# Every fourth block of one-hot columns made on ScalarE in two passes

## The chip, the cores and the metric

One NeuronCore of a Trainium2 chip. The metric is the time in microseconds that the device takes for one execution of the program. Before the change the median of three runs is 751.01 us (750.84 to 751.55).

## The reference

2048 samples, each with 40 categorical fields and 16 dense features. Every field has a table of embeddings of 32 numbers; 7 tables have 1000 rows, 10 have 1250, the others 12500 or 125000. All pairs of fields interact through a 32x32 matrix of their own, and three dense layers follow:

```python
e = jnp.stack([tbl_f[ids[:, f]] for f in range(40)], axis=1)
vi, vj = e[:, I, :], e[:, J, :]                  # 780 pairs i < j
z = jnp.einsum('bke,kef,bkf->bk', vi, W, vj)
h = jnp.concatenate([z, dense_ctx], axis=1)
h = jnp.maximum(h @ W_top1 + b_top1, 0.0)        # 796 -> 512
h = jnp.maximum(h @ W_top2 + b_top2, 0.0)        # 512 -> 256
y = h @ W_top3
```

## The kernel before

The batch is cut into four chunks of 512 samples, and the 40 fields into ten groups of four, so that a group of transposed embeddings, `e_t`, is one tile of 128 partitions by 512 samples. Seven groups are fetched by indirect DMAs that GpSimd issues (L331), are turned on TensorE (L481) and copied out of PSUM by ScalarE (L368).

The other three groups, h = 0, 1, 2, are the twelve smallest tables. They aren't fetched but looked up with matrix products. The ids of a chunk lie in `hot_sb`, the same on every partition, as fp16. For block n of 128 table rows, VectorE compares these ids with the row number of each partition and writes 1 or 0 into a tile `one_hot` (128 partitions, 4 fields, 512 samples, bf16; L425). TensorE multiplies it with the block of the table, which is kept as three bf16 parts: 12 matmuls for a block with four fields (L465), all of a group summed in the one PSUM bank `x_ps`. The groups have 8, 10 and 10 blocks, so there are 28 blocks for each chunk and 112 in all. Blocks 8 and 9 of group 1 hold one field only.

`one_hot` has three slots (HOT_SLOTS, L29). The tile of block number m goes into slot m % 3, so its maker waits until TensorE is through with block m - 3. `steps_of` (L122) writes one list of steps by hand, and every engine walks that list and does its own part in this order. In it each one-hot tile stands right behind the look-up of the block two before its own (L143 to L153). The steps of the pair products (`gen`, L484, with VectorE's multiplication at L438, and `red`, L514, which sums the products into the bank `z_ps`) fill the rest. VectorE's part of a burst of `gen` is one or two multiplications of 128x1024; TensorE and VectorE are coupled by three slots of `t_ps` and six of `prod`.

Where the look-ups stand: all 28 blocks of chunk 0 come first, one behind another, with nothing between them but ScalarE's copies of the three finished groups. The look-ups of chunk k + 1 stand between the bursts of chunk k, one or two to a burst, by the tables in `between` (L89 to L116). In chunk 0 they are spread over bursts 20 to 42, in chunks 1 and 2 they stand at bursts 25 to 29, 36 to 42 and 45 to 52. Chunk 3 has none.

When the last one-hot tile of a chunk is made, SP loads the ids of the next chunk over `hot_sb` (L305 to L309), and VectorE waits for them at the first tile of the next chunk (L415, L416).

ScalarE does the copies out of PSUM, in the order of the list: `e_t` (L368), the two hidden layers (L373, L377), and, after every eighth `red`, the full bank `z_ps` (L393). TensorE's next `red` into that bank waits for it:

```python
if s == 0 and n > 0:
    pe.wait_ge(z_read, chunk * Z_BANKS + r // Z_SLOTS)
```

Of the kernel before, what the change touches and what calls it, by code (L numbers as in the profile page):

```python
# [26 lines left out]
EARLY_TURNS = list(range(HOT_GROUPS, PER))  # L27
TABLE_PARTS = 3
HOT_SLOTS = 3  # L29

# [39 lines left out]

def hot_pieces(k, h, blocks):
    return [("hot", k, h, n) for n in range(blocks[h])]


def layer1_pieces(k, m):
# [94 lines left out]
def tower_kernel(nc, idx_lay, tables, w_lay, w1_lay, b1, w2, b2, w3, dense_t, ident_in, select_in, hot_ids,  # L172
# [18 lines left out]
    one_hots = [step[1:] for step in steps if step[0] == "one_hot"]  # L191
    one_hot_no = {s: n for n, s in enumerate(one_hots)}

    looked_up_to = {s: sum(o[2] < blocks[o[1]] - 1 for o in one_hots[:n + 1]) for n, s in enumerate(one_hots)}
    in_tail = {("h1", chunks - 1, m): m for m in range(M1)} | {("h2", chunks - 1, m): M1 + m for m in range(M2)}
    items = [(k, c) for k in range(chunks) for c in GATHERED]
# [7 lines left out]
    with ExitStack() as ctx:  # L204
# [6 lines left out]
        def sem(name):  # L211
            return ctx.enter_context(nc.semaphore(name))
# [48 lines left out]
        ids_kept = sem("ids_kept")  # L261
        hot_ids_loaded = sem("hot_ids_loaded")
        one_hot_made = sem("one_hot_made")
        looked_up = sem("looked_up")
        gathered = [sem(f"gathered{s}") for s in range(ROW_SLOTS)]
        x_made = sem("x_made")
# [10 lines left out]

        def bank_of(use):
            return t_ps[:, in_tail[use], :] if use in in_tail else x_ps[:, :]

        def e_slot(k, c):
            return item(k, c) % E_RING

        @block.sync
        def _(sp):
            sp.dma_start(idx[:, :, :], idx_lay).then_inc(idx_loaded, 16)
            for n, (first, last) in enumerate(W_PIECES):
                a, b = block_of(0, first), block_of(0, last)
                sp.dma_start(w_sb[:, a:b, :], w_lay[:, a:b, :]).then_inc(w_loaded[n], 16)
                if n == 0:  # L290
                    sp.wait_ge(ids_halved, 1)
                    sp.dma_start(hot_ids_16.rearrange("k n -> (k n)").rearrange("(p n) -> p n", p=P),
                                 ids_half[:, :]).then_inc(ids_kept, 16)
                    sp.wait_ge(ids_kept, 16)
                    sp.dma_start(hot_sb[:, :, :], hot_ids_16[0].unsqueeze(0).broadcast_to(
                        [P, HOT_GROUPS * PER * NB]).rearrange("p (f b) -> p f b", b=NB)).then_inc(hot_ids_loaded, 16)
            sp.dma_start(w1_sb[:, :, :], w1_lay).then_inc(consts, 16)
            sp.dma_start(b1_sb[:, :], b1).then_inc(consts, 16)
            sp.dma_start(b2_sb[:, :], b2).then_inc(consts, 16)
            sp.dma_start(w3_sb[:, :], w3).then_inc(consts, 16)  # L300
            sp.dma_start(w2_sb[:, :, :], w2.rearrange("(m p) n -> p m n", p=P)).then_inc(consts, 16)

            for step in steps:
                kind, k = step[:2]
                if kind == "one_hot" and step[2:] == (HOT_GROUPS - 1, blocks[-1] - 1) and k + 1 < chunks:  # L305

                    sp.wait_ge(one_hot_made, one_hot_no[step[1:]] + 1)
                    sp.dma_start(hot_sb[:, :, :], hot_ids_16[k + 1].unsqueeze(0).broadcast_to(
                        [P, HOT_GROUPS * PER * NB]).rearrange("p (f b) -> p f b", b=NB)).then_inc(hot_ids_loaded, 16)  # L309
                elif kind == "red" and step[1] % BATCHES == BATCHES - 1:  # L310

                    chunk = step[1] // BATCHES
                    bank = chunk * Z_BANKS + Z_BANKS - 1
                    sp.wait_ge(z_read, bank + 1)
                    sp.dma_start(z_sb[DENSE_AT:DENSE_AT + dense_rows, bank % Z_RING, :],
                                 dense_v[chunk]).then_inc(dense_loaded, 16)
                elif kind == "layer3" and step[2] == M2 - 1:
                    sp.wait_ge(x_taken, use_no["y", k, 0] + 1)
                    sp.dma_start(out_v[k], y_sb[:, :]).then_inc(stored, 16)
            sp.wait_ge(stored, chunks * 16)  # L320
# [17 lines left out]
        @block.scalar  # L338
        def _(act):
            act.dma_start(ids_raw[:, :], hot_ids).then_inc(hot_ids_raw, 16)  # L340
            for h in range(HOT_GROUPS):
                at = slice(block_at[h], block_at[h] + blocks[h])
                act.dma_start(tables_raw[:, at, :], hot_tables[:, at, :]).then_inc(tables_loaded[h], 16)
                if h == 0:
                    act.dma_start(row_number[:, :], row_numbers).then_inc(numbers_loaded, 16)
                    act.dma_start(ident[:, :], ident_in).then_inc(selects_loaded, 16)
                    act.dma_start(select[:, :], select_in).then_inc(selects_loaded, 16)
            act.wait_ge(hot_ids_raw, 16)
            nc.scalar.copy(ids_half[:, :], ids_raw[:, :]).then_inc(ids_halved, 1)
            for h in range(HOT_GROUPS):  # L350
                at = slice(block_at[h], block_at[h] + blocks[h])
                act.wait_ge(tables_loaded[h], 16)
                nc.scalar.copy(table_parts[:, 0, at], tables_raw[:, at, :]).then_inc(table_copied, 1)  # L353
                act.wait_ge(table_split, 2 * h + 1)
                nc.scalar.copy(table_parts[:, 1, at], tables_rest[:, 0:blocks[h], :]).then_inc(table_copied, 1)

            for step in steps:
                kind, k = step[:2]
                use, _, ends = use_of(step)
                if ends:  # L360
                    act.wait_ge(x_made, use_no[use] + 1)
                if kind in ("turn", "hot") and ends:
                    c = step[2]
                    if item(k, c) >= E_RING:

                        before = divmod(item(k, c) - E_RING, GROUPS)
                        act.wait_ge(mult_done, last_unit_with(*before) + 1)
                    nc.scalar.copy(e_t[:, e_slot(k, c), :], x_ps[:, :]).then_inc(x_taken, 1)  # L368
                elif kind == "layer1" and ends:
                    m = step[2]  # L370
                    if k == 0 and m == 0:
                        act.wait_ge(consts, CONSTS)
                    nc.scalar.activation(h1_sb[:, m, :], bank_of(use), ACT.Relu,  # L373
                                         bias=b1_sb[:, m:m + 1]).then_inc(x_taken, 1)
                elif kind == "layer2" and ends:
                    m = step[2]
                    nc.scalar.activation(h2_sb[:, m, :], bank_of(use), ACT.Relu,  # L377
                                         bias=b2_sb[:, m:m + 1]).then_inc(x_taken, 1)
                elif kind == "layer3" and ends:
                    if k:  # L380
                        act.wait_ge(stored, k * 16)
                    nc.scalar.copy(y_sb[:, :], x_ps[0:1, :]).then_inc(x_taken, 1)
                elif kind == "red":
                    chunk, r = divmod(step[1], BATCHES)
                    if r % Z_SLOTS == Z_SLOTS - 1 or r == BATCHES - 1:
                        bank = chunk * Z_BANKS + r // Z_SLOTS
                        act.wait_ge(red_done, step[1] + 1)
                        if bank >= Z_RING:

                            act.wait_ge(x_made, use_no["h1", (bank - Z_RING) // Z_BANKS, M1 - 1] + 1)  # L390
                        elif bank == 0:
                            act.wait_ge(table_split, 2 * HOT_GROUPS)
                        nc.scalar.copy(z_sb[:, bank % Z_RING, :], z_ps[:, :]).then_inc(z_read, 1)  # L393

        @block.vector
        def _(dve):
# [12 lines left out]

            for step in steps:  # L410
                kind, k = step[:2]
                if kind == "one_hot":
                    _, _, h, n = step
                    number = one_hot_no[step[1:]]
                    if h == 0 and n == 0:  # L415
                        dve.wait_ge(hot_ids_loaded, 16 * (k + 1))  # L416
                    if number >= HOT_SLOTS:

                        _, old_h, old_n = old = one_hots[number - HOT_SLOTS]
                        if old_n == blocks[old_h] - 1:  # L420
                            dve.wait_ge(x_made, use_no["e", old[0], old_h] + 1)
                        else:
                            dve.wait_ge(looked_up, looked_up_to[old])
                    used = sum(b > n for b in field_blocks[h])
                    nc.vector.tensor_scalar(one_hot[:, number % HOT_SLOTS, 0:used, :],  # L425
                                            hot_sb[:, PER * h:PER * h + used, :], row_number[:, n:n + 1], None,
# [17 lines left out]
        def _(pe):  # L444
# [8 lines left out]
            def look_up(step):  # L453
# [4 lines left out]
                    if k == 0:  # L458
                        pe.wait_ge(table_split, 2 * h + 2)
                number = one_hot_no[step[1:]]  # L460
                pe.wait_ge(one_hot_made, number + 1)
                used = sum(b > n for b in field_blocks[h])
                for part in range(TABLE_PARTS):
                    for f in range(used):
# [206 lines left out]
```

## Time and profile before

| | us |
|---|---|
| median of three runs | 751.01 |
| the profiled execution, device time | 747.58 |
| its span on the core | 745.8 |
| TensorE matmuls busy | 689.6 (92%) |
| VectorE busy | 546.2 (73%) |
| GpSimd busy | 446.0 (60%) |
| ScalarE busy | 67.2 (9%) |
| mean granted TensorE clock | 0.986 of full |

Busy is the time in which at least one instruction of the engine runs. Matmuls overlap each other, so the starts of two neighbours say more about their pace than the length of one. The look-ups of chunk 0 lie between 21.6 and 42.9 us of the span, the pair products of chunk 0 between 44.1 and about 200 us, and each later chunk takes about 180 us.

### The profile page before, as it was taken

Reading aid. Unit: us, or ns where it says so; the run is one execution under the profiler, and the core shown is the slowest. Engines: PE = TensorE matmul, PEld = TensorE weight load, DVE = VectorE, ACT = ScalarE, POOL = GpSimd, SP = SyncE. Lnnn points to the kernel's source line nnn. Section 1 sums busy time; section 2 is a strip of 40 time slices with the busy share of each in tenths; the row PEclk is TensorE's granted clock in tenths of the full one; section 3 lists DMA queues with packets and bytes.
Section 4 is the critical chain, followed back from the end, with each engine's and each line's share of the span. In section 5 each row is a group of like instructions: output and inputs, shape, how many; then the busy total and the mean of one; then the engine's idle time right before and its main releaser. Section 6 shows DMA issues by size and latency. Waiting matters only on the chain.

```text
span 745.8 us, 13215 instructions
## 1 busy us (share of the span) xinstructions
PE 689.6 (92%) x5752; PEld 199.9 (27%) x5752; DVE 546.2 (73%) x518; ACT 67.2 (9%) x104; POOL 446.0 (60%) x452
## 2 busy tenths in 40 slices
PE   0779999989999999999899999999999999999998
PEld 0322233322222223232222222222322222222222
DVE  3858999978865668698766667869886667868900
ACT  4000000000000000101000000010010000010002
POOL 6777777777777777777777777777777300000000
PEclk9999999998999999999989999999999999999999
DMA  7730000030000000000300000000000000000000
GB/s 277 278 99 14 14 14 12 15 98 13 16 14 15 15 14 14 14 13 14 98 15 15 15 14 15 13 15 12 14 15 15 8 1 1 1 1 1 1 3 1
DMA packets 18081, 23.02 MB, mean 31 GB/s; under 512 B 8356, under 2 KB 16292, under 8 KB 17256
## 3 DMA queue, kind: packets, MB, share of 16 engines
q0 software_dynamic: 14336, 7.37, 5.7%
q1 hardware_dynamic: 2680, 12.78, 4.5%
q10 hardware_dynamic: 1008, 2.04, 0.8%
q8 instruction: 45, 0.74, 0.4%
q14 instruction: 12, 0.10, 0.0%
HBM read 22.09 MB, written 0.06 MB: 30 GB/s over the span
## 4 chain that ended last, share of the span: by engine, by line
PE 73%; DVE 14%; issue 6%; DMA 3%; ACT 2%; DVEq 0%; ACTq 0%
PE t_ps L510 21%; PE z_ps L522 20%; PE x_ps L541 11%; DVE prod L438 10%; PE x_ps L465 6%; PE t_ps L499 5%; DVE one_hot L425 3%; PE t_ps L541 3%; PE x_ps L554 3%; DMA hot_sb<-hot_ids 3%; PE x_ps L481 2%; ACT e_t L368 1%; PE x_ps L565 1%; PE t_ps L554 1%; DMA z_sb<-hot_tables 1%
## 5 line engine op out<-in xcount | busy, mean ns | idle before, releaser
L438 DVE TENSOR_TENSOR prod<-t_ps,e_t 128x1024 f32<-128x1024 f32 x400 | 468.3, 1218 | 134.0 <-PE t_ps L510 99.9
L331 POOL DMA_INDIRECT rows<-tbl,idx x448 | 445.8, 995 | 140.3 <-issue 135.9
L510 PE MATMUL t_ps<-e_t,w_sb 32*128 32x512 f32 x1440 | 227.8, 642 | 9.3 <-DVE prod L438 9.3
L522 PE MATMUL z_ps<-prod,select 128*32 128x512 f32 x1600 | 218.5, 603 | 1.1 <-DVE prod L438 0.7
L510 PEld LDWEIGHTS t_ps<-e_t,w_sb 32*128 32x128 f32 x1440 | 71.3, 184 | 164.8 <-DVE prod L438 96.6
L465 PE MATMUL x_ps<-one_hot,tables 128*32 128x512 bf16 x1272 | 86.5, 386 | 28.4 <-DVE one_hot L425 25.6
L425 DVE TENSOR_SCALAR one_hot<-hot_sb,row_number 128x2048 bf16<-128x2048 f16 (+1 forms) x112 | 78.4, 733 | 17.4 <-DMA hot_sb<-hot_ids 14.8
L541 PE MATMUL x_ps<-z_sb,w_sb 128*32 128x512 f32 x672 | 89.2, 613 | 2.0 <-ACT e_t L368 2.0
L522 PEld LDWEIGHTS z_ps<-prod,select 128*32 128x32 f32 x1600 | 46.4, 110 | 101.9 <-issue 70.1
L465 PEld LDWEIGHTS x_ps<-one_hot,tables 128*32 128x32 bf16 x1272 | 29.4, 97 | 100.9 <-issue 49.3
L499 PE MATMUL t_ps<-e_t,w_sb 64*128 64x512 f32 x160 | 46.4, 656 | 4.7 <-DVE prod L438 4.7
L368 ACT COPY e_t<-x_ps 128x512 f32<-128x512 f32 x40 | 23.5, 587 | 273.8 <-PE x_ps L465 160.0
L541 PEld LDWEIGHTS x_ps<-z_sb,w_sb 128*32 128x32 f32 x672 | 14.3, 109 | 63.3 <-issue 58.3
L393 ACT COPY z_sb<-z_ps 128x512 f32<-128x512 f32 x28 | 16.4, 586 | 143.4 <-PE z_ps L522 143.4
L554 PE MATMUL x_ps<-h_sb,w_sb 128*32 128x512 f32 x192 | 24.3, 601 | 2.0 <-ACT e_t L368 2.0
L481 PE MATMUL x_ps<-ident,rows 128*128 128x128 f32 x112 | 19.3, 297 | 6.5 <-ACT e_t L368 4.1
L541 PE MATMUL t_ps<-z_sb,w_sb 128*32 128x512 f32 x224 | 24.2, 592 | 0.0
L499 PEld LDWEIGHTS t_ps<-e_t,w_sb 64*128 64x128 f32 x160 | 12.5, 191 | 39.2 <-issue 34.2
L373 ACT ACTIVATE h_sb<-x_ps,b_sb 128x512 f32<-128x512 f32 x12 | 8.2, 687 | 150.2 <-PE x_ps L541 150.2
L481 PEld LDWEIGHTS x_ps<-ident,rows 128*128 128x128 f32 x112 | 12.3, 146 | 27.3 <-issue 13.6
L541 PEld LDWEIGHTS t_ps<-z_sb,w_sb 128*32 128x32 f32 x224 | 7.3, 110 | 16.8 <-issue 16.8
L402 DVE TENSOR_TENSOR z_sb<-z_sb,tables 128x1280 f32<-128x1280 f32 (+1 forms) x3 | 4.2, 1404 | 8.5 <-ACT tables L353 8.3
(18 smaller groups left out, 46.4 us busy)
## 6 DMA issues: line engine op xcount, KB each, us to landing
rows<-tbl,idx POOLq DMA_INDIRECT x448, 2.3
hot_sb<-hot_ids SPq DMA_DIRECT2D x4, 1536.0 KB, 6.5
w_sb<-w_lay SPq DMA_DIRECT2D x1, 1792.0 KB
z_sb<-hot_tables ACTq DMA_DIRECT2D x2, 640.0 KB, 6.0
w_sb<-w_lay SPq DMA_DIRECT2D x1, 1216.0 KB
w_sb<-w_lay SPq DMA_DIRECT2D x1, 960.0 KB, 10.6
w_sb<-w_lay SPq DMA_DIRECT2D x1, 704.0 KB, 8.8
w_sb<-w_lay SPq DMA_DIRECT2D x1, 640.0 KB, 6.2
```

The lines of the kernel that those rows point to most:

```text
L331: pool.indirect_dma_start(out=rows[:, slot, t, E * f:E * f + E], out_offset=None, in_=tables[PER * c + f], in_offset=bass.IndirectOffsetOn ...
L368: nc.scalar.copy(e_t[:, e_slot(k, c), :], x_ps[:, :]).then_inc(x_taken, 1)
L393: nc.scalar.copy(z_sb[:, bank % Z_RING, :], z_ps[:, :]).then_inc(z_read, 1)
L425: nc.vector.tensor_scalar(one_hot[:, number % HOT_SLOTS, 0:used, :], hot_sb[:, PER * h:PER * h + used, :], row_number[:, n:n + 1], None, o ...
L438: nc.vector.tensor_tensor(prod[:, u % PROD_SLOTS, :, :], t_ps[:, at:at + 2, :], e_t[:, e_slot(k, c), :].unsqueeze(1).broadcast_to([P, 2, NB]),
L465: mm = nc.tensor.matmul(x_ps[E * f:E * f + E, :], tables_16[:, block_at[h] + n, part, f, :], one_hot[:, number % HOT_SLOTS, f, :], start=( ...
L481: mm = nc.tensor.transpose(x_ps[:, t * P:(t + 1) * P], rows[:, slot, t, :], ident[:, :])
L499: mm = nc.tensor.matmul(t_ps[:, at + half, :], w_sb[part, b, :], e_t[part, e_slot(k, g), :], start=True, stop=True)
L510: mm = nc.tensor.matmul(t_ps[:, at + r % 2, :], w_sb[part, b, :], e_t[part, e_slot(k, g), :], start=True, stop=True)
L522: mm = nc.tensor.matmul(z_ps[E * q:E * q + E, :], select[:, E - PER - PER * s:2 * E - PER - PER * s], prod[:, u % PROD_SLOTS, q % 2, :], s ...
L541: mm = nc.tensor.matmul(into[E * q:E * q + E, :], w1_sb[:, kb, m * P + E * q:m * P + E * q + E], z_sb[:, bank % Z_RING, :], start=first, s ...
L554: mm = nc.tensor.matmul(into[E * q:E * q + E, :], w2_sb[:, j, m * P + E * q:m * P + E * q + E], h1_sb[:, j, :], start=first, stop=ends)
```

## The change

A tile of one-hot columns is made by ScalarE instead of VectorE where its block number is 3 or 7 within its group: 6 of the 28 tiles of each chunk, 24 of 112 in all, every one with four fields. ScalarE computes |row - id| into the slot and then, over the same slot, max(0, 1 - that). Between the two passes it waits for its own semaphore. Makers now count on two semaphores, `one_hot_made` (VectorE) and `one_hot_acted` (ScalarE); TensorE waits for the one that belongs to the tile, and SP's reload of `hot_sb` waits for both. The order of the steps is as before.

```diff
+SHARE = 4
+def on_scalar(one_hot):
+    return one_hot[2] % SHARE == SHARE - 1
@@ SP, reload of the ids
-                    sp.wait_ge(one_hot_made, one_hot_no[step[1:]] + 1)
+                    done = one_hots[:last_made[k] + 1]
+                    sp.wait_ge(one_hot_made, sum(not on_scalar(o) for o in done))
+                    sp.wait_ge(one_hot_acted, sum(on_scalar(o) for o in done))
@@ ScalarE, in its walk over the steps, ahead of the copies
+                if kind == "one_hot" and on_scalar(step[1:]):
+                    _, _, h, n = step
+                    number = one_hot_no[step[1:]]
+                    act.wait_ge(numbers_loaded, 16)
+                    act.wait_ge(hot_ids_loaded, 16 * (k + 1))
+                    wait_for_slot(act, number)
+                    used = sum(b > n for b in field_blocks[h])
+                    slot = one_hot[:, number % HOT_SLOTS, 0:used, :]
+
+                    nc.scalar.activation(slot, hot_sb[:, PER * h:PER * h + used, :], ACT.Abs,
+                                         bias=row_number[:, n:n + 1], scale=-1.0).then_inc(one_hot_near, 1)
+                    act.wait_ge(one_hot_near, made_to[step[1:]])
+                    nc.scalar.activation(slot, slot, ACT.Relu, bias=1.0, scale=-1.0).then_inc(one_hot_acted, 1)
@@ VectorE
-                if kind == "one_hot":
+                if kind == "one_hot" and not on_scalar(step[1:]):
@@ TensorE, look-up
-                pe.wait_ge(one_hot_made, number + 1)
+                pe.wait_ge(one_hot_acted if on_scalar(step[1:]) else one_hot_made, made_to[step[1:]])
```

`wait_for_slot` holds the wait for the slot that stood in VectorE's part before, and is now used by both makers.

## Rows read from the trace of the kernel before

**Rows 1.** The page, its first part: busy time of each engine.

```profile
PE 689.6 (92%) x5752; PEld 199.9 (27%) x5752; DVE 546.2 (73%) x518; ACT 67.2 (9%) x104; POOL 446.0 (60%) x452
```

**Rows 2.** Groups by shape: busy us, mean ns of one, idle before.

```profile
L425 DVE TENSOR_SCALAR one_hot<-hot_sb,row_number 128x2048 bf16<-128x2048 f16 x104 | 75.7, 760 | 17.2 <-DMA hot_sb<-hot_ids 14.8 <-PE x_ps L465 2.4
L368 ACT COPY e_t<-x_ps 128x512 f32<-128x512 f32 x40 | 23.5, 587 | 273.8 <-PE x_ps L465 160.0 <-PE x_ps L481 113.8
L373 ACT ACTIVATE h_sb<-x_ps,b_sb 128x512 f32<-128x512 f32 x12 | 8.2, 687 | 150.2 <-PE x_ps L541 150.2
L353 ACT CAST tables<-z_sb 128x1280 bf16<-128x1280 f32 x2 | 2.5, 1254 | 0.0
L349 ACT ACT_TABLE_LOAD x1 | 1.3, 1283 | 4.2 <-issue 4.2
L353 ACT CAST tables<-z_sb 128x1024 bf16<-128x1024 f32 x1 | 1.0, 1044 | 1.4 <-DMA z_sb<-hot_tables 1.4
```

**Rows 3.** Waits of the whole span: us in total, times, longest.

```profile
PE x_ps L465 <- DVE one_hot L425: 25.6, 12, 21.6
```

**Rows 4.** Timeline of the look-ups of chunk 0: start us, length us.

```profile
21.57 6.62 PE L465 MATMUL x_ps<-one_hot,tables 128*32 128x512 bf16 x96 [21.57 <-DVE one_hot L425]
23.09 0.75 DVE L425 TENSOR_SCALAR one_hot<-hot_sb,row_number 128x2048 bf16<-128x2048 f16 x1 [0.34 <-PE x_ps L465]
28.24 0.59 ACT L368 COPY e_t<-x_ps 128x512 f32<-128x512 f32 x1 [9.01 <-PE x_ps L465]
41.84 0.34 SPq L308 DMA_DIRECT2D hot_sb<-hot_ids  x1
48.35 1.42 DVE L425 TENSOR_SCALAR one_hot<-hot_sb,row_number 128x2048 bf16<-128x2048 f16 x2 [6.54 <-DMA hot_sb<-hot_ids]
```

**Rows 5.** The same stretch, TensorE's weight loads alone.

```profile
23.66 0.18 PEld L465 LDWEIGHTS x_ps<-one_hot,tables 128*32 128x32 bf16 x4 [0.24 <-issue]
24.08 2.97 PEld L465 LDWEIGHTS x_ps<-one_hot,tables 128*32 128x32 bf16 x56 [0.24 <-issue]
```

**Rows 6.** TensorE in four stretches: from:to, length, busy us, granted clock (PEclk), DMA.

```profile
51.00:54.40 3.40, 3.35 (x12) 0.57 0.09 16
168.00:172.00 4.00, 3.25 (x12) 0.50 0.05 9
...
217.79:221.70 3.91, 2.81 (x20) 1.00 0.09 17
221.70:225.10 3.40, 3.15 (x16) 0.56 0.10 15
```

**Rows 7.** Timeline of TensorE, look-ups of chunk 1 among the bursts of chunk 0.

```profile
99.29 0.83 PE L465 MATMUL x_ps<-one_hot,tables 128*32 128x512 bf16 x12
101.98 0.83 PE L465 MATMUL x_ps<-one_hot,tables 128*32 128x512 bf16 x12
...
147.09 0.83 PE L465 MATMUL x_ps<-one_hot,tables 128*32 128x512 bf16 x12
150.01 0.83 PE L465 MATMUL x_ps<-one_hot,tables 128*32 128x512 bf16 x12
```

**Rows 8.** Timeline of chunk 1, group 0 of the look-ups for chunk 2.

```profile
281.34 1.48 PE L465 MATMUL x_ps<-one_hot,tables 128*32 128x512 bf16 x24 [0.67 <-ACT e_t L368]
284.68 1.48 PE L465 MATMUL x_ps<-one_hot,tables 128*32 128x512 bf16 x24
289.77 0.59 ACT L393 COPY z_sb<-z_ps 128x512 f32<-128x512 f32 x1 [8.48 <-PE z_ps L522]
294.14 0.83 PE L465 MATMUL x_ps<-one_hot,tables 128*32 128x512 bf16 x12 [0.87 <-DVE one_hot L425]
```

**Rows 9.** Timeline of chunk 1, group 1 of the look-ups for chunk 2.

```profile
317.57 1.48 PE L465 MATMUL x_ps<-one_hot,tables 128*32 128x512 bf16 x24
319.98 0.59 ACT L393 COPY z_sb<-z_ps 128x512 f32<-128x512 f32 x1 [3.52 <-PE z_ps L522]
321.56 1.03 PE L522 MATMUL z_ps<-prod,select 128*32 128x512 f32 x8
```

More of the change, by code:

```diff
@@ L192, in tower_kernel @@
     one_hot_no = {s: n for n, s in enumerate(one_hots)}
+    made_to = {s: sum(on_scalar(o) == on_scalar(s) for o in one_hots[:n + 1]) for n, s in enumerate(one_hots)}
+    last_made = {k: max(n for n, o in enumerate(one_hots) if o[0] == k) for k in range(chunks)}
     looked_up_to = {s: sum(o[2] < blocks[o[1]] - 1 for o in one_hots[:n + 1]) for n, s in enumerate(one_hots)}
@@ L263, in tower_kernel @@
         one_hot_made = sem("one_hot_made")
+        one_hot_near = sem("one_hot_near")
+        one_hot_acted = sem("one_hot_acted")
         looked_up = sem("looked_up")
@@ L279, in bank_of, with wait_for_slot @@
             return t_ps[:, in_tail[use], :] if use in in_tail else x_ps[:, :]
+        def wait_for_slot(engine, number):
+            if number >= HOT_SLOTS:
+                _, old_h, old_n = old = one_hots[number - HOT_SLOTS]
+                if old_n == blocks[old_h] - 1:
+                    engine.wait_ge(x_made, use_no["e", old[0], old_h] + 1)
+                else:
+                    engine.wait_ge(looked_up, looked_up_to[old])
         def e_slot(k, c):
@@ L416, in _ @@
                         dve.wait_ge(hot_ids_loaded, 16 * (k + 1))
[L417 to L423, printed above, removed]
+                    wait_for_slot(dve, number)
                     used = sum(b > n for b in field_blocks[h])
```

## The prediction

> **What bounds the kernel now.** I read the busy times first. TensorE is busy 92% of the span, VectorE 73%, ScalarE 9% [rows 1]. The change takes work from the second and gives it to the idlest, so the question is where VectorE is what TensorE waits for, and where a slow maker would be waited for instead. Next the waits. The look-ups wait 25.6 us for one-hot tiles, but 21.6 of these are the one wait before the first tile, which the change doesn't touch; 4.0 us are left over the whole run [rows 3]. VectorE's lateness also shows as a slower pace. Where one look-up stands in each burst, two neighbours start 2.69 us apart while VectorE keeps up, and 2.92 us apart later in the chunk, where it makes two multiplications and one tile for each burst and runs without a gap [rows 7]. So VectorE is the bound by 0.23 us in such bursts, and TensorE nearly everywhere else. Walking the three look-up stages of a chunk burst by burst and subtracting TensorE's own pace, I find 4.0 us lost in chunk 0 and about 4 us in each of chunks 1 and 2. These 12 us are the most that a quicker VectorE can give back there.
>
> **What a tile costs on each engine.** VectorE takes 0.76 us for a tile of 128x2048 [rows 2]; in an unbroken row they start 0.66 to 0.7 us apart, which is what VectorE gets back for each tile. ScalarE has no operation of this size or with fp16 in. Its casts take 1.044 us for 1024 columns and 1.254 for 1280, so 0.82 ns a column, and 1.88 us at 2048. A bias read from a column adds 0.10 us (0.687 against 0.587) [rows 2]. I take 1.98 us a pass and, with the wait between the passes and the hand-over at both ends (0.05 us each, as other hand-overs in the timeline), 4.1 us from a free slot to a usable tile. Bounds: 0.74 us a pass if ScalarE went through 2-byte data as VectorE does, 2.1 if anything is added. The nearest rows are ScalarE's own, and the value is taken from them.
>
> The Trainium skill (ScalarE: Activation LUTs, Rules for kernel authors) says to use VectorE and not ScalarE for simple functions such as relu and max, with VectorE up to about three times as fast on bf16. The rows above make one pass 2.6 times as long as VectorE's whole tile, and there are two; so the trace agrees, and the rule speaks against the change, though not against moving work that is hidden.
>
> **Part 1, the look-ups of chunk 0.** Here nothing stands between the blocks. The tile of block m can be begun when block m - 3 is through, and is wanted when m - 1 is. TensorE runs a block in 0.64 us (14 groups of four weight loads in 2.97 us, so 0.212 us a third of a block) [rows 5], and the last results come 0.19 us after the next block can start (0.83 us in rows 7). So a maker has about 2 x 0.64 - 0.19 = 1.1 us. VectorE fits, ScalarE with 4.1 us does not: each of its six tiles here (numbers 3, 7, 11, 15, 21, 25) stops TensorE for about 3 us. No other work hides it.
>
> The chain, at full clock: block 0 is through at 23.03, as VectorE's start at 23.09 shows [rows 4]. Number 3 is ready at 27.2. Blocks 3 and 4 run (1.48 us) and free the slot for 7, ready 5.6 us on, at 32.8. Then block 7, the copy of group 0 (0.59 us [rows 4], some 0.7 with hand-overs), block 8, number 11: 6.5 us, 39.3. Number 15 is ready at 44.9. Blocks 15 to 17, a copy, block 18 and number 21: 7.8 us, 52.6. Number 25 is ready at 58.2. At that moment the reload of the ids can start, because SP now waits for ScalarE's tiles too. It started at 41.84 before, and VectorE went on 6.5 us later at 48.35 [rows 4]; TensorE waited for that anyway. So chunk 0 starts its pair products 58.2 - 41.8 = 16.4 us later. Of the three copies, none waits behind a tile here, since each stands ahead of the next tile in ScalarE's order.
>
> Then the clock. The first blocks start their thirds 0.43 us apart, twice as long as from 24.08 on [rows 5]: the engine at 1.2 GHz instead of 2.4. Later the granted clock is at or near half for some microseconds at 51.0 (after 4.7 us without work), at 168 (around an idle time of 3.4 us) and at 221.7, where only 1.1 us of the 3.9 before had been idle [rows 6]. The new stops of 2.4 to 2.9 us in every 5.6 lie between these, so TensorE will often be at half clock here. What lies on the chain are the 12 blocks that run between a ready tile and the next free slot (2, 2, 2, 4, 2); each costs 0.64 us more at half clock, 7.7 us for all. I take three quarters, 5.8 us, since they follow right behind the stops; bounds 0 and 7.7. Part 1: 16.4 + 5.8 = 22.2 us later.
>
> **Part 2, chunk 0's bursts.** Look-ups stand 2.7 to 2.9 us apart, mostly one to a burst. A tile is wanted two such distances after the block ahead of it began, even where blocks 0 and 1 share a burst: 2 x 2.69 - 0.19 = 5.2 us from the end of block 0 to the start of block 3 at 101.98 [rows 7], against 4.1 us. All six tiles are in time, and the one bank copy that falls behind a tile (in group 1) is wanted only by a `red` behind four more look-ups. VectorE loses 6 x 0.66 = 4.0 us of work, TensorE had 4.0 us to get back; the two don't meet in every burst, so I take 3.0 us saved, bounds 0 and 4.0.
>
> **Part 3, chunks 1 and 2.** The same in each:
> - Group 0 has two look-ups to a burst. Block 0 is through at 282.2, ScalarE's tile 3 is ready at 286.3, and TensorE wants it at 284.68 + 0.65 = 285.3 [rows 8]: 1.0 us stop. Tile 7 stands behind the copy of `z_ps` (289.77 + 0.59), so it is ready 4.1 us later at 294.45, plus the 1.0 us shift; TensorE started that block at 294.14, after 0.87 us of waiting for VectorE [rows 8]. Another 0.3 us lost, 0.2 got back behind it. Together 1.1 us slower.
> - Group 1: ScalarE starts tile 3 at 318.45 (block 0 of 317.57 + 0.83 us) and is done at 322.55. The copy of the full `z_ps`, which ran at 319.98, is queued behind it and ends at 323.1; the `red` that began at 321.56 needs it [rows 9]. Stop of 1.6 us, less 0.6 us that VectorE had cost in this stage: 1.0 slower. Tile 7 is in time.
> - Group 2: both tiles in time (distances 5.2 and 5.8 us), the copy of the bank stands before. Some 1.2 of 2.2 us are got back.
>
> Sum 1.1 + 1.0 - 1.2, about 1.0 us slower in each chunk, 2.0 for both; bounds are 8 us saved in all if nothing is late, 10 lost if every tile of groups 0 and 1 stops TensorE for 1.2 us. Chunk 3 has no look-ups, and its time stays. The waits of TensorE on another semaphore cost nothing, being one for one.
>
> **Sum.** 22.2 - 3.0 + 2.0 = 21.2 us. The profiled execution, 747.58 us, would become 768.8. It lies 3.4 us under the median of the runs, which I keep as an offset: 751.0 + 21.2 = 772.2 us.
>
> **The rivals.**
> - TensorE keeps its full clock in part 1. For it: idle times up to 0.87 us are followed by full clock elsewhere; against it the stretch before 221.7. Time 751.0 + 16.4 - 1.0 = 766.4. Chance 0.2.
> - Faster: ScalarE's pass on 2-byte data is as quick as VectorE's, 0.74 us. A tile is then usable 1.65 us after its slot is free. Part 1 costs 6 x (1.65 - 1.1) = 3.3 us, and all tiles among bursts are in time, so that up to 12 us come back, 8 by my measure of part 2 (three quarters of 12, less the last tiles). 751.0 + 3.3 - 8 = 746. It decides from about 1 us a pass down: there part 1 costs 6 us, and parts 2 and 3 give as much. No row of ScalarE is near that rate; chance 0.03, with 0.02 for a time within 0.2%.
> - The two functions need different tables. One table load takes 1.283 us [rows 2], and there would be two to a tile. Part 1 alone grows by 6 x 2.57 = 15.4 us, the tiles of parts 2 and 3 come late by another 1 to 2.5 us each (18 of them, say 25 us in all): some 812. The trace has one load for copies, casts and relu together; it has no abs. Chance 0.03. In a sentence by itself: the Trainium skill (ScalarE: Activation LUTs, Table sets: the hidden batching unit) puts relu, copy and abs in every set as filler, by which this can't happen; the trace bears it out for relu and copy.
> - The delay of part 1 is hidden behind the gathers or the weights. GpSimd is busy for 446 us [rows 1] and never makes TensorE wait in the timeline of chunk 0, where its groups arrive 5 us or more before they are turned; a later start only widens that. Nothing to hide behind; no chance of its own.
>
> **How the numbers follow.** Forecast 0.72 (part 1 with a clock mostly at half), rival 1 0.2, rival 2 with its neighbourhood 0.05, rival 3 0.03. The likeliest is the forecast, 772.2 us. The range takes in rival 1 with a few us more saved in parts 2 and 3, and the forecast with all 12 blocks at half clock and some tiles late: 762 to 781. What a measurement of this kernel can tell from no change is about 0.2%, 1.5 us. Faster 0.03, same 0.02, slower 0.95.
>
> **What would show it.** ScalarE's two new groups at about 1.98 us each, x24, no second table load. In the look-ups of chunk 0, five or six waits of TensorE of 2.4 to 2.9 us for ScalarE's tile, and the reload of the ids at 58 us (full clock) to 66 (half clock) instead of 41.84. VectorE busy some 18 us less. In chunks 1 and 2 a `red` that waits about 1.6 us for the copy of its bank. I am wrong if a pass is far from 1.98 us, if TensorE's pieces keep 0.21 us, or if late copies stop it at more places than the two of part 3.

## The result

The changed kernel takes 767.7 us (767.0 to 768.55, four runs), the one before 750.9 us (750.1 to 751.6) beside it. The ratio is 1.0224, 95% interval 1.0207 to 1.0242: clearly slower. The forecast was 772.2 us, in a range of 762 to 781. The profiled execution took 768.55 us against 747.58 before, 21.0 us more; the medians are only 16.8 us apart, as the profile of before lies 3.3 us under the median of its runs and that of after 0.9 above. The accounts by place further down are of the two profiles, so of 21 us; what makes the 4 us between the two differences was not traced.

| | before | after |
|---|---|---|
| median, us | 750.9 | 767.7 |
| profiled execution, us | 747.58 | 768.55 |
| TensorE busy, us | 689.6 | 694.1 |
| VectorE busy, us | 546.2 | 533.7 |
| ScalarE busy, us | 67.2 | 160.4 |
| mean granted clock | 0.986 | 0.980 |

The groups of after that make the tiles, by shape (busy us, mean ns of one, idle before). They answer to the first line of [rows 2]:

```profile
L454 DVE TENSOR_SCALAR one_hot<-hot_sb,row_number 128x2048 bf16<-128x2048 f16 x80 | 61.2, 776 | 40.3 <-PE x_ps L494 24.2 <-DMA hot_sb<-hot_ids 16.0
L391 ACT ACTIVATE one_hot<-hot_sb,row_number 128x2048 bf16<-128x2048 f16 x24 | 48.1, 2003 | 56.3 <-PE x_ps L494 56.3
L394 ACT ACTIVATE one_hot<-one_hot 128x2048 bf16<-128x2048 bf16 x24 | 45.9, 1911 | 0.8
```

The two passes take 2.00 and 1.91 us, so ScalarE's tile costs five times VectorE's 0.78. VectorE itself now idles 24.2 us in front of its own tiles, waiting for slots that TensorE frees late. TensorE's waits over the whole span of after (us in total, times, longest) show for what:

```profile
PE x_ps L494 <- DVE one_hot L454: 23.4, 5, 21.5
PE x_ps L494 <- ACT one_hot L394: 16.8, 10, 2.8
PE z_ps L551 <- ACT z_sb L428: 2.5, 2, 1.3
```

VectorE's part has fallen from 25.6 [rows 3] to 23.4, of which 21.5 is the first wait. Two new waits, 19.3 us together, have come for the 2.2 us that went. The timeline of after, TensorE and ScalarE in the look-ups of chunk 0 (start, length, what, idle before; lines between left out), shows where most of it lies. It answers to [rows 4]:

```profile
21.49 4.03 PE L494 MATMUL x_ps<-one_hot,tables 128*32 128x512 bf16 x36 [21.49 <-DVE one_hot L454]
23.10 2.00 ACT L391 ACTIVATE one_hot<-hot_sb,row_number 128x2048 bf16<-128x2048 f16 x1 [3.94 <-PE x_ps L494]
...
25.13 1.91 ACT L394 ACTIVATE one_hot<-one_hot 128x2048 bf16<-128x2048 bf16 x1
...
27.09 4.24 PE L494 MATMUL x_ps<-one_hot,tables 128*32 128x512 bf16 x48 [1.57 <-ACT one_hot L394]
...
33.97 1.47 PE L494 MATMUL x_ps<-one_hot,tables 128*32 128x512 bf16 x12 [2.64 <-ACT one_hot L394]
...
41.73 2.77 PE L494 MATMUL x_ps<-one_hot,tables 128*32 128x512 bf16 x48 [1.57 <-ACT one_hot L394]
...
47.34 3.70 PE L494 MATMUL x_ps<-one_hot,tables 128*32 128x512 bf16 x18 [2.83 <-ACT one_hot L394]
...
56.67 4.46 PE L494 MATMUL x_ps<-one_hot,tables 128*32 128x512 bf16 x48 [2.83 <-ACT one_hot L394]
...
62.88 2.13 PE L494 MATMUL x_ps<-one_hot,tables 128*32 128x512 bf16 x36 [1.75 <-ACT one_hot L394]
62.92 0.34 SPq L330 DMA_DIRECT2D hot_sb<-hot_ids  x1
```

Six stops, one for each of ScalarE's tiles, 13.2 us in all. Three last 2.6 to 2.8 us, as forecast, and three only 1.57 to 1.75 us, as the blocks that run meanwhile ran at half pace. ScalarE starts the first at 23.10, when block 0 is through, and TensorE takes it up at 27.09: 4.0 us. Where the runs of matmuls are long for their number (4.24 us for 48 against 2.77 for another 48) TensorE goes at half pace in part of them; from 33 us on the granted clock shows it too (rows further down). For blocks 3 and 4 only the pace shows it, as the granted clock reads 1.00 between 26 and 30 us. The reload of the ids starts with the last tile, at 62.92 instead of 41.84.

The starts of the same steps in both profiles (TensorE's turns of gathered groups, which don't change their place) give the delay that has piled up. Each start of before is subtracted from its partner of after:

| up to | before, us | after, us | delay, us | forecast |
|---|---|---|---|---|
| first turn of chunk 0 | 43.55 | 65.70 | 22.15 | 22.2 for part 1 |
| TensorE's restart behind the reload | 51.05 | 72.02 | 20.97 | |
| turn behind burst 8 | 67.44 | 89.58 | 22.14 | |
| turn behind burst 51 (end of part 2) | 170.75, 190.92 | 190.41, 210.51 | 19.6 | -3.0 for part 2 |
| chunk 1, behind group 0 | 306.62 | 327.15 | 20.5 | +1.1 |
| chunk 1, behind group 1 | 337.77 | 359.35 | 21.6 | +1.0 |
| chunk 2, first turns | 402.40 | 422.12 | 19.7 | -1.2 |
| chunk 3, first turns | 575.35 | 595.94 | 20.6 | +1.0 for the chunk |
| end of the span | 745.8 | 766.7 | 20.9 | 21.2 |

### The profile page after: what moved, and what is told of

It reads as the page before. It is cut to its first block, busy times and chain, and to the rows that moved or that the text cites. A ratio compares the mean times of both kernels' runs of the same rounds, so it can differ in the third digit from the quotient of the medians.

```text
span 766.7 us, 13266 instructions
## 1 busy us (share of the span) xinstructions
PE 694.1 (91%) x5752; PEld 197.6 (26%) x5752; DVE 533.7 (70%) x494; ACT 160.4 (21%) x152; POOL 441.1 (58%) x452
## 4 chain that ended last, share of the span: by engine, by line
PE 73%; DVE 9%; ACT 8%; issue 5%; DMA 3%; DVEq 0%; ACTq 0%; SPq 0%
PE t_ps L539 21%; PE z_ps L551 20%; PE x_ps L570 11%; DVE prod L467 7%; PE x_ps L494 6%; PE t_ps L528 5%; ACT one_hot L391 3%; PE t_ps L570 3%; PE x_ps L583 3%; ACT one_hot L394 3%; DMA hot_sb<-hot_ids 3%; PE x_ps L510 2%; DVE one_hot L454 1%; ACT e_t L403 1%; PE x_ps L594 1%
## 5 line engine op out<-in xcount | busy, mean ns | idle before, releaser
L353 POOL DMA_INDIRECT rows<-tbl,idx x448 | 440.9, 984 | 140.3 <-issue 135.6
L539 PE MATMUL t_ps<-e_t,w_sb 32*128 32x512 f32 x1440 | 223.2, 642 | 9.8 <-DVE prod L467 9.8
L494 PE MATMUL x_ps<-one_hot,tables 128*32 128x512 bf16 x1272 | 95.4, 413 | 42.9 <-DVE one_hot L454 23.4
L539 PEld LDWEIGHTS t_ps<-e_t,w_sb 32*128 32x128 f32 x1440 | 67.3, 184 | 165.5 <-DVE prod L467 109.3
L454 DVE TENSOR_SCALAR one_hot<-hot_sb,row_number 128x2048 bf16<-128x2048 f16 (+1 forms) x88 | 64.4, 744 | 41.2 <-PE x_ps L494 25.1
L391 ACT ACTIVATE one_hot<-hot_sb,row_number 128x2048 bf16<-128x2048 f16 x24 | 48.1, 2003 | 56.3 <-PE x_ps L494 56.3
L403 ACT COPY e_t<-x_ps 128x512 f32<-128x512 f32 x40 | 23.4, 586 | 170.2 <-PE x_ps L510 112.6
L394 ACT ACTIVATE one_hot<-one_hot 128x2048 bf16<-128x2048 bf16 x24 | 45.9, 1911 | 0.8
L570 PE MATMUL t_ps<-z_sb,w_sb 128*32 128x512 f32 x224 | 24.2, 592 | 0.0
```

Of the source, the lines that this page charges most:

```text
L353: pool.indirect_dma_start(out=rows[:, slot, t, E * f:E * f + E], out_offset=None, in_=tables[PER * c + f], in_offset=bass.IndirectOffsetOn ...
L391: nc.scalar.activation(slot, hot_sb[:, PER * h:PER * h + used, :], ACT.Abs, bias=row_number[:, n:n + 1], scale=-1.0).then_inc(one_hot_near, 1)
L394: nc.scalar.activation(slot, slot, ACT.Relu, bias=1.0, scale=-1.0).then_inc(one_hot_acted, 1)
L494: mm = nc.tensor.matmul(x_ps[E * f:E * f + E, :], tables_16[:, block_at[h] + n, part, f, :], one_hot[:, number % HOT_SLOTS, f, :], start=( ...
L539: mm = nc.tensor.matmul(t_ps[:, at + r % 2, :], w_sb[part, b, :], e_t[part, e_slot(k, g), :], start=True, stop=True)
L570: mm = nc.tensor.matmul(into[E * q:E * q + E, :], w1_sb[:, kb, m * P + E * q:m * P + E * q + E], z_sb[:, bank % Z_RING, :], start=first, s ...
```

## The experiments

Two theories stood against each other. Mine: the cost is a chain in the unbroken look-ups of chunk 0, as long as ScalarE's tile less the two blocks that run meanwhile, with half clock on top. The rival: ScalarE's tiles cost wherever they are, by late copies, hand-overs or contention.

**A first set, disturbed by the chips.** Five runs with all gathers in place ran on two chips where the kernel before itself took 1175 to 1195 us. Windows of 140 us of TensorE (length, busy us and instructions of PE, PEld, DVE, ACT, POOL, clock), first of the original profile of before, then of the same kernel on such a chip:

```profile
60.00:200.00 140.00, 134.18 (x1086) 40.84 (x1082) 124.42 (x121) 9.39 (x16) 107.48 (x107) 0.98 0.11 25
```

```profile
60.00:200.00 140.00, 6.92 (x24) 1.08 (x24) 3.08 (x4) 0.00 (x0) 106.15 (x112) 0.50 0.09 13
```

GpSimd issues its gathers as before, and TensorE gets through 24 matmuls instead of 1086, with the idle time put down to its own issue. Behind the last gather, from 900 us on, it runs at its usual pace. Waits for tiles are then mixed with waits for its own issue: in e1 the reload of chunk 0 starts at 241.4 us instead of 41.8. No forecast of a reload time was met in this set, and it says little about the change.

e1_before_again is the kernel before, unchanged.

> The kernel before, once more. The profiled execution of before took 747.6 us, its timed runs 750.1 to 751.6, while after's runs and its profile agree (767.0 to 768.6). Theory: TensorE's clock falls at somewhat different places from run to run, so this profile may have more half-clock stretches than the first one and a time of 750 to 751 us; ratio 1.000. Rival: the first trace is typical, 747.6 again, and the profile itself runs 3 us faster than timed runs.

Measured: 1189.9 us, ratio 1.0021 (0.9977 to 1.0065). It tells nothing on the 3 us between the first profile and the runs, since the regime is another. On a third chip the kernel before took 747.4 to 751.6 us in 17 runs, median 749.3. The first profile's 747.6 lies at the low end of that scatter. The slower executions have no trace, but their mean granted clocks are on record: the five at 0.986 took 747.4 to 748.7 us, the three at 0.982 took 750.4 to 751.3. So they most likely differ in how long the clock is at half; this was not tested.

e2_first_chunk_only:

```diff
-    return one_hot[2] % SHARE == SHARE - 1
+    return one_hot[0] == 0 and one_hot[2] % SHARE == SHARE - 1
```

> ScalarE makes only the six tiles of chunk 0, VectorE all others. Theory (the cost lies in the unbroken look-ups of chunk 0): the reload of the ids starts at 62 to 63 us as after the change, the later chunks run as before, and the profile is about 21 us over the profile of before, the timed ratio 1.023 to 1.028. Rival (the cost is spread over ScalarE's late copies in all chunks): less than half of it, ratio under 1.012.

Measured: 1202.9 us, ratio 1.0187 (1.0125 to 1.0248), between the two forecasts. The reload starts at 249.6 us, 8.2 later than in e1, and TensorE waits 35.6 us in all for ScalarE's tiles. e3_later_chunks_only is the other half:

```diff
-    return one_hot[2] % SHARE == SHARE - 1
+    return one_hot[0] > 0 and one_hot[2] % SHARE == SHARE - 1
```

> VectorE makes all tiles of chunk 0, ScalarE its 18 tiles of the later chunks. Theory: the reload stays at 41.8 us; 2.5 us are saved among the bursts of chunk 0 and about 1.3 us lost in chunks 1 and 2 together: ratio 0.997 to 0.999. Rival (late copies and late tiles cost as much as VectorE gains, or more): ratio 1.000 to 1.005.

Measured: 1185.6 us, ratio 1.0007 (0.9973 to 1.0041), so neither side is told apart. e4_fill puts work of no use ahead of TensorE's six waits:

```diff
+                if k == 0 and on_scalar(step[1:]):
+                    for _ in range(FILL):          # FILL = 12
+                        nc.tensor.matmul(t_ps[:, 0, 0:3 * P], tables_16[:, 0, 0, :, :]..., tables_16[:, 0, :, :, :]...,
+                                         start=True, stop=True)
```

> The change whole, and ahead of each of TensorE's six waits for ScalarE's tile in chunk 0 twelve matmuls of 128x384 whose result nobody reads (1.9 us at full clock, 3.8 at half, in a stop of 2.4 to 2.9 us). Theory (some 4.7 of the 21 us of chunk 0's look-ups come from half clock behind the stops): the stretch 24 to 60 us is at full clock, the reload starts at 58 to 59 us instead of 62.9, ratio about 1.017. Rival (the clock has no part in it, the chain is ScalarE's alone): reload at 62.9 or later, ratio 1.022 or more.

Measured: 1201.9 us, ratio 1.0177 (1.0114 to 1.024), with the reload at 250.9. The ratio is the one forecast, but its interval takes in the rival's 1.022 as well, and e2's is the same within the scatter. e5_one_pass drops ScalarE's second pass:

```diff
-                                         bias=row_number[:, n:n + 1], scale=-1.0).then_inc(one_hot_near, 1)
-                    act.wait_ge(one_hot_near, made_to[step[1:]])
-                    nc.scalar.activation(slot, slot, ACT.Relu, bias=1.0, scale=-1.0).then_inc(one_hot_acted, 1)
+                                         bias=row_number[:, n:n + 1], scale=-1.0).then_inc(one_hot_acted, 1)
```

> The change whole, but ScalarE's second pass is left out, so that its tiles hold |row - id| and not 1 or 0 and the result isn't the reference's. A tile is then usable some 2.1 us after its slot is free instead of 4.1. Theory (the stop is the tile's time less the two blocks in between): six chain links of chunk 0's look-ups each 2.0 us shorter, less half clock, reload of the ids at 47 to 49 us; tiles and bank copies in chunks 1 and 2 in time; time within 3 us of before, ratio 0.996 to 1.004. Rival (the hand-over to ScalarE itself costs, whatever the tile takes): still 8 us or more slower, ratio over 1.010.

Measured: 1190.3 us, ratio 1.0034 (0.9999 to 1.007), with the reload at 244.0: the ratio is as forecast, the reload is not. Even on these chips the tiles of chunk 0 alone cost 1.9%, those of the later chunks nothing that can be measured, and one pass instead of two little, which leans to my theory; but that is all.

**A second set, without gathers.** As TensorE's slow issue went with the gathers, all further kernels leave them out: GpSimd fills the rows once, and nothing else changes for the other three engines.

```diff
-            pool.wait_ge(idx_loaded, 16)
-            for n, (k, c) in enumerate(items):
-                ...
+            nc.gpsimd.memset(rows[:, :, :, :], 0.5).then_inc(rows_filled, 1)
@@ turn
-                pe.wait_ge(gathered[slot], (rounds + 1) * GATHER)
+                pe.wait_ge(rows_filled, 1)
```

g1_before:

> The kernel before without its gathers: GpSimd fills the rows once with a constant and issues no DMA, so the result isn't the reference's; TensorE, VectorE and ScalarE do the same work in the same order. In the runs with gathers here TensorE got its instructions only every 0.7 us or slower while GpSimd was issuing gathers. Theory: without them the timeline is that of the first profile, 744 to 752 us. Rival: TensorE's slow issue has nothing to do with the gathers, and the time stays over 1000 us.

Measured: 746.1 us (745.6 to 746.5), on a chip where the kernel before with its gathers took 1182.6 beside it. So the gathers were what TensorE's issue suffered from there, and g1 is a fair stand-in: its look-ups of chunk 0 begin at 21.5 us, its first turn is at 44.42, its reload at 42.71. That is 0.9 later than in the profile of before, as the first blocks ran longer at the slow pace. g1 to g4 ran on the same chip.

g2_after:

> The kernel after the change, without its gathers (result not the reference's). Against the same without the change. Theory: 17 to 22 us longer, reload of the ids at 62 to 64 us instead of 41.8, stops of TensorE for ScalarE's tile in chunk 0 as in the profile of after. Rival (part of the cost came from ScalarE's tiles beside gathers): under 12 us.

Measured: 767.5 us (765.3 to 769.4), 21.4 more. Reload at 62.94; the waits for ScalarE's tiles are the same 16.8 us in ten waits, to the tenth.

g3_first_chunk_only, with the edit of e2:

> Without gathers (result not the reference's), ScalarE makes only the six tiles of chunk 0. Theory (the whole cost lies in the unbroken look-ups): the same reload time as the full change, 62 to 64 us, and at the end 1 to 2 us MORE than the full change, since the 2.5 us saved among chunk 0's bursts are gone and only 1.3 us of losses in chunks 1 and 2. Rival: clearly less than the full change, by 5 us or more.

Measured: 764.9 us (761.0 to 766.5), 18.8 over g1 and 2.6 under g2. Reload at 65.16, later than forecast: its first block began 1.2 us later than in g2, and blocks 11 and 12 ran at half clock too. The delay to g1 is 23.5 us at the first turn, 20.8 at the start of chunk 1 (212.86 against 192.11) and stays 20.6 to the end of the span. So nearly all of the cost does lie in chunk 0's look-ups, but the order that I expected between g3 and g2 came out the other way. Some 2 us of g3's delay went at the end of chunk 0, around the next wait for ids, where it has the half clock for 3.4 us and g1 for 6.8. From the start of chunk 1 to the end g2 lost 5 us against g1 and g3 nothing. The late tiles and copies, less what VectorE's relief gave back, make about half of these 5; another 1.7 is a stretch of half clock in chunk 3, which no tile of ScalarE's touches. Differences of 2 us between such runs aren't safe to read.

g4_fill:

> Without gathers (result not the reference's), the full change, and ahead of each of TensorE's six waits for ScalarE's tile in chunk 0 twelve matmuls of 128x384 whose result nobody reads. Theory (4.7 us of the cost are half clock behind the stops): look-ups at full clock from the second stop on, reload at 58 to 59.5 us, 3 to 5 us less than the full change. Rival (ScalarE's chain alone sets it): no gain, reload at 62.9 or later.

Measured: 762.8 us (761.8 to 765.2), 4.7 less than g2, both forecasts met. Granted clock of TensorE from 24 us on, g4 first, then g2 (from:to, length, busy us, clock, DMA):

```profile
24.00:60.00 36.00, 30.74 (x350) 1.00 0.17 65
```

```profile
24.00:63.00 39.00, 24.44 (x266) 0.82 0.16 62
```

```profile
25.45 2.88 PE L481 MATMUL t_ps<-tables 128*128 128x384 bf16 x12
28.25 2.77 PE L488 MATMUL x_ps<-one_hot,tables 128*32 128x512 bf16 x48
30.96 2.12 PE L481 MATMUL t_ps<-tables 128*128 128x384 bf16 x12
```

These last lines are g4's timeline. With filled stops the clock stays full and 48 matmuls take 2.77 us where they took 4.24. The first filling is by its length (2.88 us against 2.12) still partly at half pace, which the granted clock of its row doesn't show, and pushes block 3 from 27.10 to 28.25, 1.15 us; the reload is at 59.35, 3.6 us earlier. Together the clock's share of the look-ups is 4.7 us. The rest, 16.4 us of chain (59.35 - 1.15 - 41.84, the reload of before; 15.5 against g1's own 42.71), stays with a clock that is full: useless work beside it saves time, and the wait itself remains. That the medians are 4.7 us apart too is partly chance: the two profiles end 7.6 us apart, 3.6 of it at the reload, the rest by other stretches of half clock behind it.

g5_four_slots:

```diff
-ROW_SLOTS = 10
+ROW_SLOTS = 9
-HOT_SLOTS = 3
+HOT_SLOTS = 4
```

> Without gathers (result not the reference's), the full change with four slots for the tiles in place of three, so that each tile can be begun one block earlier (the rows get nine slots in place of ten, for room). Theory (lateness is the tile's 4.0 us against the time from a free slot to its use): by the same chain number 3 stops nothing and number 25 is ready at 52 us at full clock, reload at 52 to 55 instead of 62.9; no late tile and no late bank copy in chunks 1 and 2; 750 to 756 us in all, against 767.5 with three slots. Rival (ScalarE's tiles cost by contention or hand-over, not by distance): within 4 us of 767.5.

Measured: 751.8 us (749.8 to 752.7), 15.7 less than g2. g5, g6 and g7 ran on the third chip, the one where the kernel with its gathers takes 749.3 (750.9 on the first), so a difference of 1 or 2 us to g1 or g2 may be the chip's. For g5 that is too little to touch the reading. The reload is at 52.80, as forecast, and TensorE's waits are now:

```profile
PE x_ps L482 <- DVE one_hot L442: 21.4, 1, 21.4
PE t_ps L527 <- DVE prod L455: 10.2, 7, 4.4
PE x_ps L482 <- ACT one_hot L382: 9.9, 5, 2.2
```

Five stops of 1.7 to 2.2 us, all in chunk 0; the first tile, which finds an empty slot, stops nothing, no bank copy is late, and the clock kept its full rate in the look-ups. Tiles of the same price do much less harm when they can be begun one block earlier; some 6 us over g1 are left.

g6_in_time_only:

```diff
-    return one_hot[2] % SHARE == SHARE - 1
+    k, h, n = one_hot
+    return n % SHARE == SHARE - 1 and (k == 1 or (k > 1 and (h == 2 or (h == 1 and n == 7))))
```

> Without gathers (result not the reference's), ScalarE makes only the tiles that were in time and delayed nothing: all six that are made for chunk 1, and for chunks 2 and 3 block 7 of group 1 and blocks 3 and 7 of group 2. Theory: reload as before at 42 us, 2 to 3 us saved in chunk 0 and about 1.5 in each of chunks 1 and 2, so 739 to 743 us against 746.1 without the change. Rival (VectorE's relief isn't worth anything where TensorE is the bound, the saving in after was the clock's): 745 to 747.

Measured: 741.9 us (740.1 to 743.2), 4.2 under g1. The profiles show where, with 0.8 us aside, by which g6's first block began earlier: 0.4 us saved by the look-ups of groups 0 and 1 in chunk 0, 2.4 in group 2 and around the reload behind it, then about 1.5 us in each of chunks 1 and 2; against these, 1.7 us lost at 220 us by a stretch of half clock that g1 doesn't have. Of the 2.4 part is the clock's, as g6 has the half clock for 3.4 us at that reload and g1 for 6.8. TensorE never waits for a tile of ScalarE's. That is with the gathers left out and between two chips, so it isn't a run of the whole kernel, and the size is not safe to 2 us; the pattern of the choice is what it supports.

g7_one_pass, with the edit of e5:

> Without gathers, the full change less ScalarE's second pass (its tiles hold |row - id|; result not the reference's). A tile is usable some 2.1 us after its slot is free. Theory (stop = the tile's time less the two blocks between): each of six chain links 2.0 us shorter, half clock only at the first, reload at 46 to 49 us; nothing late in chunks 1 and 2; 743 to 750 us. Rival (the number of stops counts, or the hand-over, whatever their length): over 755.

Measured: 743.9 us (743.5 to 744.9). The reload is at 46.77, as forecast, and the stops of chunk 0 are down to 0.9 us each:

```profile
PE x_ps L480 <- ACT one_hot L379: 4.5, 5, 0.9
```

So a stop is as long as the tile less the two blocks: 2.8 us for a tile of 3.9 to 4.0 at full clock, 0.9 for one of 2.0. With one pass the time is even 2.2 us under g1's (on the other chip): by the rival's reading, that the stops or the hand-overs cost whatever the tile takes, it would have stayed over 755.

## Why the prediction was right, and where it was off

**Part 1 was right in mechanism, and its chain to a tenth.** ScalarE's six first passes start 6.9, 7.8, 5.6, 9.3 and 6.2 us apart in after. Forecast for full clock were 5.6, 6.5, 5.6, 7.8 and 5.6, and from the second on g4, with its stops filled, has just these: 6.5, 5.6, 7.8, 5.6. The difference, 4.7 us, is the clock's part of the chain, where I had taken 5.8: the blocks at half pace are 3, 4, 7, 8, 15, 16, half of 17 and nearly all of 22, some 7.4 of the 12 that I named, against the 9 that I took.

That the delay of the first turn, 22.15 us, is the forecast's 22.2 to a tenth is luck. By my own sum, chain and clock, it would be 16.4 + 4.7 = 21.1, and that is by how much the reload is later (62.92 against 41.84); VectorE goes on 21.0 later (69.32 against 48.35), and so does TensorE behind it. The first turn is 22.15 later because more of the look-ups is left for TensorE when the last tiles are made (2.8 us from the reload to the turn, 1.7 before). By the turn behind burst 8 the delay is 22.14 again for another reason: behind the wait for the ids the clock is at half for 6.8 us where it was for 3.4 ([rows 6], 51.0 to 54.4 us):

```profile
70.70:77.60 6.90, 5.58 (x20) 0.53 0.08 14
```

Neither was in the sum.

The granted clock in the look-ups of after was 0.52 (33.3 to 40.1), 0.54 (46.9 to 50.3) and 0.55 (57.1 to 60.5):

```profile
33.30:40.10 6.80, 5.44 (x48) 0.52 0.09 15
40.10:43.50 3.40, 1.83 (x40) 0.96 0.11 15
43.50:46.90 3.40, 1.01 (x20) 1.00 0.08 12
46.90:50.30 3.40, 2.96 (x17) 0.54 0.08 14
50.30:57.10 6.80, 3.29 (x47) 0.98 0.09 15
57.10:60.50 3.40, 3.40 (x40) 0.55 0.09 15
```

The rival with a full clock is refuted by these rows; its time of 766.4 is nevertheless nearer to the measured median than mine, by accident.

**Part 2, 3.0 us saved, was sized too high.** From the start of the first block of a group to that of its last, before and after: group 0 15.47 and 15.31 us, group 1 18.57 and 18.57, group 2 21.69 and 20.49. With 0.24 us behind the last block of group 0, VectorE's relief gave 1.6 us, not 3.0. The rest of the 2.5 us comes around the reload, where the half clock lasted from 167.1 to 173.9 before and only from 190.2 to 193.7 after:

```profile
167.10:170.50 3.40, 1.75 (x4) 0.56 0.08 14
170.50:173.90 3.40, 3.40 (x16) 0.50 0.06 11
```

```profile
186.80:190.20 3.40, 0.84 (x4) 1.00 0.07 12
190.20:193.70 3.50, 3.50 (x16) 0.55 0.10 14
```

The length of that stretch isn't the change's doing: g2 has the change and 6.8 us of half clock there, g3 has the tiles of the kernel before in these bursts and 3.4. The step that failed is "three quarters of 4.0" (the recorded 3.0): I summed what TensorE lost and what VectorE would save over the chunk, though the two must meet in the same burst. They did so mainly in group 2, where one look-up to a burst runs on for long and the pace was 2.92 us [rows 7]; it is 2.69 in most bursts of after and once 2.92. All six tiles were in time, as forecast. VectorE's busy time fell by 12.5 us, not by the 18 that I gave as a sign: its 80 tiles of full size that are left are busy for 61.2 us against 75.7 for 104, so the 24 that went gave back 14.5, and each of the others takes 0.776 us instead of 0.760.

**Part 3 was right place by place, its total of 2.0 came out at 1.0.** Chunk 1 of after (the answers to [rows 8] and [rows 9]):

```profile
305.90 0.83 PE L494 MATMUL x_ps<-one_hot,tables 128*32 128x512 bf16 x12 [0.79 <-ACT one_hot L394]
314.82 0.83 PE L494 MATMUL x_ps<-one_hot,tables 128*32 128x512 bf16 x12 [0.99 <-ACT one_hot L394]
343.54 1.06 PE L551 MATMUL z_ps<-prod,select 128*32 128x512 f32 x8 [1.27 <-ACT z_sb L428]
```

The late tile 3 of group 0 stops TensorE for 0.79 us (forecast 1.0), tile 7 behind the bank's copy for 0.99 in place of VectorE's 0.87, and the `red` behind the late bank copy for 1.27 (forecast 1.6). The delay grows by 0.9 and 1.05 us over the two groups, where I had 1.1 and 1.0. Group 2 gave back 1.27 us from its first to its last block (21.37 to 20.10), forecast 1.2. Some 0.6 us more came back in chunk 1 by a shorter half clock at its reload (371.9 to 378.7 before, 394.9 to 398.4 after), so the chunk as a whole cost 0.1 instead of 1.0; chunk 2, which has no reload behind it, cost 0.9.

**The offset was the largest error of the time.** Against its own profile the sum was 768.8 us and the profile took 768.55; that is closer than the parts deserve, as 0.5 us too much saved in part 2 and 0.35 us at the end of the span that no part had stand against 1.0 us too much lost in part 3. I then carried 3.4 us over, from the profile of before to the median of its runs. After's profile and its runs agree within 1.6 us, so the offset didn't carry over: 772.2 against 767.7. The change of the medians is 16.8 us where I had 21.2. The step that failed is that one number for "profile against runs" was taken to hold for both kernels; what makes it up in the kernel before stays open, as none of its slower runs has a trace.

**The other rivals.** ScalarE's pass was 2.0 us and not 0.74, so there was no gain; g7 shows that the condition was rightly named, as with a tile of 2.0 us the loss is gone (2.2 us under g1), and g5 that a slot more leaves 5.7 us of it. There was one table load in after, no more; here the Trainium skill (ScalarE: Activation LUTs, Table sets: the hidden batching unit), which has abs and relu in every set, was borne out. The rule of the Trainium skill that simple functions belong on VectorE (ScalarE: Activation LUTs, Rules for kernel authors) holds here for chunk 0, but not for tiles that are in time: g6 moved 12 and was 4.2 us faster than g1, across two chips.

## What to carry to other kernels

A slower maker is free only as long as its whole latency fits between the moment when its slot comes free and the moment when the tile is wanted; its share of busy time says nothing about that. Do the sum for each stage, also for the one at the start where nothing runs beside it, and look at what is queued behind the new work on the engine that takes it. To move work off an engine pays only in the bursts in which that engine is what is waited for: choose the tiles one by one, and give them a slot more where there is room. Don't add the distance between one profile and its runs to a forecast as if it were a constant.

## What the runs showed of the hardware

- Among stops of 1.6 to 2.8 us, one behind another, TensorE fell to half clock in parts of a stage (0.52 to 0.55 in the rows above). To fill them with useless matmuls kept it at 1.00 and saved 4.7 us of 767.5. g5's stops of 1.7 to 2.2 us and g7's of 0.9 left it at 1.00 in the same stage.
- Stretches of half clock lie at different places and have different lengths from run to run, also where the work is the same: at the wait for ids at the end of chunk 0 they last 6.8 us in before, g1 and g2 and 3.4 in after, g3 and g6 (0.9 us of time between before and after), and at 220 us g6 has 3.4 us of it where g1 has none (1.7 us of time).
- On two chips TensorE's issue nearly stood still while GpSimd was issuing indirect DMAs: 24 matmuls in 140 us instead of 1086, and 1187 us in all instead of 751. Without the gathers it took 746.1 on one of them. On a third chip the kernel took 749.3 with its gathers. What sets this off was not found.
- ScalarE's two passes over 128x2048 took 2.00 us (fp16 in, bias from a column of the kernel's) and 1.91 us (bf16 in place). What makes the 0.09 us between them wasn't tried.
